# An attention and routed feed-forward kernel: the experts' weights split one pass later, the first table's steps spread over three passes, v's product moved behind the maxima's turn in the last passes

## What is computed

```python
# attention with 16 heads of 16, local: row i sees rows i-64 .. i
q, k, v = split(x @ W_attn + b_attn)
scores = einsum('bhtd,bhsd->bhts', q, k) / sqrt(16), masked
x = layernorm(x + softmax(scores) @ v @ W_proj + b_proj)
# each row goes to one of 8 experts, then a shared output weight
e = argmax(x @ Wr.T)
inter = gelu(x @ W1[e] + b1[e])
y = inter @ Wo + bo + x
y = (y - mean) * rsqrt(var + 1e-12) * gamma + beta
x = layernorm(x + y)
```

## Time and profile before

| | us |
|---|---|
| median of 3 runs (lowest, highest) | 550.52 (549.26, 554.35) |
| the profiled execution | 547.5 |
| its span, first to last instruction | 545.5 |
| PE busy | 494.5 |
| DVE busy | 421.4 |
| ACT busy | 353.8 |
| POOL busy | 320.6 |

### The profile page before, as it was taken

How to read it: one execution, slowest core, us unless ns; L and a number is a source line. 1 busy time by engine, 2 the same in 40 slices (tenths; PEclk the granted TensorE clock), 3 DMA queues, 4 the chain that set the end, 5 groups by cost and what they waited for, 6 DMA issues and landing times. The chain is left out here.

```text
span 545.5 us, 24637 instructions
## 1 busy us (share of the span) xinstructions
PE 494.5 (91%) x8593; PEld 435.1 (80%) x8593; DVE 421.4 (77%) x1117; ACT 353.8 (65%) x800; POOL 320.6 (59%) x570
## 2 busy tenths in 40 slices
PE   4579999999999999989897899898999999999890
PEld 3458888888888888878786689897999999999780
DVE  3437888898788885886886647899999999888583
ACT  3437777768686785674756487665667667677560
POOL 7801444445453464443526456788888888888584
PEclk9959999999999997997988999999999999999896
DMA  9697676787786968687567112222343266244510
GB/s 209 166 240 190 169 205 183 225 236 183 205 217 184 248 188 219 178 227 175 145 163 194 37 42 80 61 81 71 93 100 96 81 218 228 81 146 156 179 27 14
DMA packets 97353, 83.72 MB, mean 153 GB/s; under 512 B 37447, under 2 KB 88784, under 8 KB 97235
## 3 DMA queue, kind: packets, MB, share of 16 engines
q1 hardware_dynamic: 93874, 73.70, 49.7%
q0 software_dynamic: 3264, 8.41, 4.5%
q10 hardware_dynamic: 96, 0.04, 0.0%
HBM read 43.63 MB, written 23.62 MB: 123 GB/s over the span
## 5 line engine op out<-in xcount | busy, mean ns | idle before, releaser
L1683 PE MATMUL ps<-wo_hi,ks 128*128 128x256 f16 x576 | 129.5, 274 | 4.3 <-DVE ks L1269 4.0
L1701 PE MATMUL ps<-sT_hi,w_hi 128*128 128x128 f16 x496 | 104.9, 220 | 0.4 <-issue 0.4
L1701 PE MATMUL ps<-sT_lo,w_hi 128*128 128x128 f16 x496 | 105.0, 220 | 0.0
L1701 PE MATMUL ps<-sT_hi,w_lo 128*128 128x128 f16 x496 | 105.0, 220 | 0.0
L1146 DVE TENSOR_REDUCE mx<-ps 128x4 bf16<-128x512 f32 x128 | 82.7, 683 | 8.8 <-PE ps L1469 8.2
L666 POOL CAST att_hi<-att 128x256 f16<-128x256 f32 x32 | 12.7, 396 | 123.9 <-DVE att L974 123.9
L1683 PE MATMUL ps<-wo_lo,ks 128*128 128x256 f16 x288 | 78.8, 274 | 0.0
L816 ACT ACTIVATE probs<-ps 128x512 f32<-128x512 f32 x128 | 69.4, 612 | 6.6 <-PE ps L1495 5.9
L1372 PE MATMUL ps<-v_even,probs 128*64 128x17 f32 x1024 | 71.5, 212 | 1.4 <-issue 1.4
L1372 PE MATMUL ps<-v_odd,probs 128*64 128x17 f32 x1024 | 71.5, 212 | 0.3 <-issue 0.3
L1372 PEld LDWEIGHTS ps<-v_even,probs 128*64 128x64 f32 x1024 | 66.8, 141 | 5.1 <-issue 4.5
(11 more groups left out here) (266 smaller groups left out, 1531.4 us busy)
## 6 DMA issues: line engine op xcount, KB each, us to landing
qk_s<-qk_hi SPq DMA_DIRECT2D x64, 128.0 KB, 3.0
w_in<-in_L_ffn_W_dram SPq DMA_DIRECT2D x32, 256.0 KB, 4.0
v_odd<-slots SPq DMA_DIRECT2D x62, 128.0 KB, 2.1
qs<-qk_s SPq DMA_DIRECT2D x16, 384.0 KB, 4.3
ks<-qk_s SPq DMA_DIRECT2D x16, 384.0 KB, 5.2
ks<-qk_s SPq DMA_DIRECT2D x32, 144.0 KB, 3.9
v_even<-v_odd SPq DMA_DIRECT2D x63, 68.0 KB, 4.2
qk_s<-qk_lo SPq DMA_DIRECT2D x32, 128.0 KB, 3.5
```

The source lines that it names most:

```text
L1683: ins = mm(ps_y[p], h[p][hs][:, ic, :], wo[ws][:, ic, :], start=n == 0, stop=n == 3 * IC - 1)
L1701: up_ins = mm(ps_h[1 - p][:, half, col + m * width:col + (m + 1) * width], weights(ws, owners[m], k, ic), sT[1 - p][ss][:, k, at], start=k ...
```

## The change

Three things change.

- The experts' weights: SP issues the load of unit it+2 in pass it (before: unit it+3, and units 0 and 1 together in pass -2), ACT casts unit it in pass it (before: it+1), and DVE splits unit it in pass it (before: it+1). In pass 31, the split stands behind maxima(0) and maxima(1).
- The first table's eleven steps on DVE are done five in pass 26 and three in pass 27, both behind qk_lo, and three in pass 28 ahead of attT's copy. In pass 28 write_table comes ahead of taken_early.
- In passes 28 to 30 PE makes v's product behind the maxima's turn, and turns the attention behind scores_t(1). The order of ACT is not changed there.

```diff
@@ sync
-                for n in (0, 1) if it == -2 else (it + 3,) if a_tile(it + 3) and it > -2 else ():
+                n = it + 2
+                if a_tile(n):
 
                     cols = slice(n % 2 * I // 2, (n % 2 + 1) * I // 2)
                     wait(sp, w1l_done, n - 1)
@@ scalar
-                n = it + 1
+                n = it
                 if a_tile(n):
                     piece, cols = n // 2, slice(n % 2 * I // 2, (n % 2 + 1) * I // 2)
                     act.wait_ge(w1_ld[n % 2], 16 * (n // 2 + 1))
@@ vector
-            def early_runs():
...
-            def early_entries():
...
+            def early_table(it):
+
+                if it == EARLY_OF + 2:
+                    dve.wait_ge(table_consts, 1)
+                    dve.wait_ge(place_done, EARLY_OF // 2)
+                    link(nc.vector.tensor_tensor(total[:, :], place[1 - EARLY_OF // 2 % 2][:, 2, :], region_at[:, :],
+                                                 ALU.subtract))
+                    whole_runs()
+                    link(nc.vector.tensor_tensor_scan(runs_to[:, 1:E + 1], ones_e[:, 0:E], runs[:, 0:E], 0.0, ALU.mult, ALU.add))
+                if it == EARLY_OF + 3:
+                    link(nc.vector.scalar_tensor_tensor(shift[:, 0:E], runs_to[:, 0:E], -float(P), begin[:, 0:E],
+                                                        ALU.mult, ALU.add))
+                    nc.vector.tensor_tensor(adds[:, 0, 0:E - 1], shift[:, 1:E], shift[:, 0:E - 1], ALU.subtract)
+                    link(nc.vector.tensor_scalar(passed[:, 0:E - 1], runs_to[:, 1:E], entry_no[:, :], None, ALU.is_le))
+                if it == EARLY_OF + 4:
...
@@ vector, in the pass
+                def low_weights(n):
+
+                    piece, cols = n // 2, slice(n % 2 * I // 2, (n % 2 + 1) * I // 2)
+                    dve.wait_ge(w1h_done, n + 1)
+                    nc.vector.scalar_tensor_tensor(w1s[1][:, piece, cols], w1_in[:, cols], W_UP,
+                                                   w1s[0][:, piece, cols], ALU.mult, ALU.subtract)\
+                        .then_inc(w1l_done, 1)
+
                 maxima(0)
                 maxima(1)
+                if it == LAST:
+                    low_weights(it)
...
                     router_x(it + 1)
+                if it == EARLY_OF + 4:
+                    early_table(it)
                 if a_tile(done):
                     dve.wait_ge(attT_done, done + 1)
                     wait(dve, proj_done, done)
                     nc.vector.tensor_copy(attT[:, :, :, :], ps_attT).then_inc(attT_out, 1)
-                n = it + 1
-                if a_tile(n):
...
+                if a_tile(it) and it < LAST:
+                    low_weights(it)
                 if a_tile(old) and old % 2 == 1:
                     slots_of(pair)
-                if it == EARLY_OF + 2:
-                    early_runs()
-                    early_entries()
                 if it == EARLY_OF + 4:
+                    write_table(0, 0, EARLY)
                     taken_early()
-                    write_table(0, 0, EARLY)
...
+                if it < EARLY_OF + 4:
+                    early_table(it)
@@ tensor
-                if a_tile(it + 1):
-                    m = it + 1
+                ending = it >= TILES - LEAD
+
+                def v_product(m):
+
...
+                if a_tile(it + 1) and not ending:
+                    v_product(it + 1)
...
                 queries_keys(range(2 * CC))
                 if it == LAST:
                     first_up(first_owner, range(IC // 4, IC // 2))
+                elif ending:
+                    v_product(it + 1)
                 elif a_tile(done):
                     turn_attention(done, ps_attT)
...
-                if it == LAST:
+                if ending:
                     turn_attention(done, ps_attT)
                 scores_t(2)
                 scores_t(3)
```

More of the change, by code:

```diff
@@ L1044, in early_entries @@
-            def early_entries():
[L1046 to L1054, removed]
+            def early_table(it):
[12 more added lines that the diff above has]
+                if it == EARLY_OF + 4:
+                    link(nc.vector.tensor_tensor(added[:, :, 0:E - 1], passed[:, 0:E - 1].unsqueeze(1).broadcast_to([P, 2, E - 1]),
+                                                 adds[:, :, 0:E - 1], ALU.mult))
+                    link(nc.vector.tensor_reduce(entry[0][:, :], added[:, :, 0:E - 1], AX.X, ALU.add))
+                    nc.vector.scalar_tensor_tensor(entry[0][:, 0:1], entry_no[:, :], float(P), entry[0][:, 0:1],
+                                                   ALU.mult, ALU.add).then_inc(entries_known, 1)
```

## The result

| | before | changed |
|---|---|---|
| median (lowest, highest) of 21 runs each, same chips | 548.75 (539.5, 559.69) | 556.39 (547.12, 562.16) |
| ratio, changed to before | | 1.0133, 95% interval 1.0086 to 1.018 |
| the profiled execution, its span | 547.5, 545.5 | 556.41, 554.6 |
| mean granted clock of the span | 0.953 | 0.940 |

The change makes the kernel slower by 1.3%, 7.3 us. Single executions of one kernel spread over some 20 us, so a ratio here leaves out those far above the kernel's fastest.

A forecast was written before the change was run, and what follows sets the result against it. PE, busy 91% of the span, was taken to bound the kernel. Terms -2.9 - 2.8 + 2.9 + 2.7 + 0 + 0.4 = +0.3 us moved the median from 550.5 to 550.8, range 546.0 to 556.5.

The forecast's parts named there:

- Within 1%: Whole kernel: the outcome "same", neither under 545.0 nor over 556.0 us; chance 0.73.
- the first rival: From pass 28, PE stands 2 to 3 us each pass, clock stays 1.2 GHz through pass 31: +5 to +9, 557.5; chance 0.15.
- A, the start: Passes -1 and 0: weights one pass later, so PE goes on at 29.05 instead of 31.97: -2.9 us.
- B, the table: Passes 26 to 28: qk_lo goes ahead of the table's steps, PE does not wait for it: -2.8 us.
- C, v's product: Passes 28 to 30: product behind the maxima's turn delays ACT's rows and scores_t, +1.1 us a pass: +2.9 us net.
- D, SP's order: Passes 29 and 30: x's last rows queue behind unit 31's load, PE stands at L1527: +2.7 us, bounds 0.5 and 4.
- E, the clock: Passes 28 to 30: new low-clock stretches cost 2.7 us, offset by 2.7 already lost before: 0, bounds -3.4 and +4.
- F, pass 31: Pass 31: DVE splits unit 31 between its maxima and sT_lo, after ACT's cast: +0.4 us, bounds 0 and +1.

The follow-up runs named there:

- the stand filled: Changed kernel with x's last rows loaded ahead of the weights on SP, plus 24 unread matmuls behind v's product in passes 28 to 30: 550.27 us, ratio 1.0015.
- the old ending with rows first: Changed kernel with the old PE order of passes 28 to 30 and, on SP, x's last rows loaded ahead of the weights: 545.93 us, ratio 0.9913.
- ACT's order mended: Changed kernel with ACT writing the first half of the maxima's rows ahead of v's copy in passes 28 to 30: 548.97 us, ratio 0.9997.
- the one with rows first: Changed kernel, its new ending kept, with SP issuing x's last rows' loads ahead of the weights in pass 29: 552.97 us, ratio 1.0066.
- both orders mended: Changed kernel with ACT's first maxima's rows ahead of v's copy and x's last rows loaded ahead of the weights: 541.97 and 548.97 us, ratios 0.9849 and 0.9967.
- the filled one of the first group: Changed kernel with 24 matmuls on ready tiles, results unread, behind v's product in passes 28 to 30: 555.67 us, ratio 1.0106.

## Why the prediction was right in its number and wrong in its course

The time, 556.39, lies inside the range by 0.1 us, which is luck. The forecast was a change of +0.3 us from a median of 550.5, taken from three runs; the change was +7.3 us, from 548.75 in 21 runs. Against the value named it is only 5.6 too much since before's median came out lower. "Within 1%" (the likeliest) did not happen: it was the first rival, to which the prediction gave 0.15 and 557.5 us. By its steps:

- **A, the start (-2.9): right.** The transpose starts at 28.57 (said: 29.05). Turn of pass 0: 35.02 for 38.41, -3.4; at the turn of pass 2 it is -1.8, where PE waits 0.73 us for keys. The weights alone gave -2.7 at pass 0 and -2.8 at pass 2, so the giving back is of one profile: in the mean the turn of pass 2 stands at 57.0 us in the three profiles with the old weights (55.8 to 58.0) and at 54.3 in the eleven with the new ones (51.9 to 56.5), -2.7.
- **B, the table (-2.8): right.** No wait for qk_lo in pass 27 and no 0.50 there; the step of the earlier trace rows fell from 10.9 to 9.0 us. PE waits about 0.5 three times for DVE's maxima, as charged once. Net -2.1 to the turn of pass 28; in the mean 20.2 us from the turn of pass 26 in the three profiles with the old table and 17.6 in the eleven with the new one, -2.6.
- **C, v's product (+2.9): mechanism and size right at full clock.** With the stand filled, turn 29 to 30 takes 307.61 - 298.56 = 9.05 us, in the old ending with rows first 8.08 (287.63 to 295.71): +0.97, where the forecast had +1.1 a pass. The wait of 1.51 for the rows is there in all three passes.
- **D, SP's order (+2.7): right at full clock,** where the stand took 2.23 to 2.47 us in four versions. In the changed kernel it took 1.36, since PE is at 1.2 GHz before it; the prediction's lower bound had this case with 0.5.
- **E, the clock (0): the step that failed.** It gave D's stand one stretch of 3.4 us and C's three stands together half a chance of one more, though the earlier trace rows has one of 3.4 and one of 6.8, and set what before loses there against it. (That loss it put at 2.0 us; half of the 5.83 us that PE was busy there is 2.9.) The stretches were 20.5 and 10.2 us. In time at 0.50 that is 30.7 us against 6.8: (30.7 - 6.8) / 2 = 12 us, where the turns show +10.8 in all. The waits of C and D hardly come on top of it, as far as length times clock tells, which did not grow.
- **F, pass 31 (+0.4): right, as far as can be told.** From the turn of pass 31 to the end the changed kernel takes 232.1 us and, in its second profile, 231.0, for before's 230.9. In the mean it is 231.4 in the eleven profiles with this edit (230.8 to 232.4) and 230.9 in the three without it (230.8 to 231.1), +0.4, which is less than single profiles of one kernel differ by.

The prediction priced the rival nearly right, by a pass's PE work at half speed (13 us; measured 12.8, 13.4, 13.1), and set the point from which it decides at 14 us. What it lacked was a reason for its chance. Its "against" was that the longer stretch of the earlier trace rows was over in pass 30; but there only the old waits for att_lo followed (0.96 and 1.11 us before 297.03 and 307.14), and here a stand of 1.51 came in each pass.

That ACT's stands keep the clock down is shown: with the three stands of 1.51 us the stretch that began at the turn of pass 28, or in that pass, held for 20.5, 13.6, 20.5 and 17.1 us in four profiles; with ACT's order mended, or the stand filled, the low clock that began there lasted 6.8 us at most, in five profiles, and in three of them there was none. The Trainium skill (TensorE: Matmul & The Clock Gate, "A second HAM failure mode") speaks of frequent short idles between groups of matmuls that make the clock swing; the rows agree in that frequent short stands go with a low clock, but here the clock did not swing back for 20.5 us.

What stays open is why it starts where it does. In the changed kernel and in the one with rows first, 0.50 begins at the turn of pass 28, at 283.8 and 280.9, before the first stand of 1.51 us begins (at 284.8 and 282.4), so that stand did not bring the fall; just ahead lie only waits for DVE's maxima of 0.45 to 0.58. With ACT's order mended, and with rows first and the stands filled, it fell at the same turn too. The two profiles with both orders mended, and the filled one of the first group, have these waits without a fall there. Also open is why the same stand for x's rows was followed by 6.8, 10.2 and 20.5 us at 0.50, and the one of 2.19 for attT by none; no run varied the length of the stand alone.

## What to carry to other kernels

When an edit makes the bounding engine stand some 1.5 to 2.5 us, price the clock behind it too, and give it a chance of its own: here 1.51 us in each of three passes cost 8.9 and 9.8 us against versions at full clock, and one wait of 2.2 to 2.4 us cost 4.7 and 9.0 against the same two, but not every stand brought a fall. Before moving a producer later, look at each in-order queue behind it for the instruction that waits for it, and at what stands behind that one: two moves of a few lines each (ACT's copy behind the first rows, SP's row loads ahead of the weights) turned +1.3% into -0.3 and -1.5% in two measurements. And time the parts of a bundled change apart: the table's steps alone gave -0.7%, and with the weights one pass later and the rows first -0.9%.

## What was not expected of the hardware

- The granted clock stayed at 0.50 for 20.5 us with PE busy for 19.3 of 20.3 us (weights only). Once it worked again, PE's longest stand in that time was 0.31 us.
- A stand does not always bring a fall: three waits of 1.05 to 1.41 us for att_lo, in the old ending with rows first, left the clock at 1.00 over 26.2 us, and so did the one of 2.19 us in the filled version with rows first.
- Between the turns of passes 2 and 26, where no edit changes the order of a pass, single profiles of these versions took 207.7 to 216.1 us, with stretches of 0.50 in different places. That is a spread of 8 us that no edit made, and why the turns of passes 28 and 31 told the versions apart better than the medians.
